# A selective-scan megakernel: GpSimd makes every fourth product of dt*u with B, in place, and those scans read SBUF alone

## The chip, the cores and the metric

One core of one Trainium2 chip. The metric is the device time of one execution in microseconds (us); the median of several executions counts. The times shown here come from three timed executions of the kernel before and from one profiled execution.

## What is computed

The input is eight sequences of 512 tokens with 128 channels, float32. Two layers follow each other for each sequence: a bidirectional Mamba block with a feed-forward part, a gated ternary MLP, an attention layer with low-rank keys and values, and a mixture of eight experts with top-2 gates. The change touches only the recurrence of the Mamba block:

```
def _selective_scan(u, dt, A, Bm, Cm, Dp):
    h0 = jnp.zeros((u.shape[0], D_INNER, D_STATE), u.dtype)

    def step(h, inp):
        u_t, dt_t, B_t, C_t = inp
        dA = jnp.exp(dt_t[:, :, None] * A)
        h = dA * h + (dt_t * u_t)[:, :, None] * B_t[:, None, :]
        y = jnp.einsum('bds,bs->bd', h, C_t)
        return (h, y)
    _, ys = lax.scan(step, h0, (...))
    return ys.transpose(1, 0, 2) + u * Dp
```

It runs once forwards and once backwards in time, each with 256 inner channels and 16 states, so there are 4096 recurrences of 512 steps for each direction and sequence.

## The kernel before, in words

**Units.** 128 recurrences (8 channels with 16 states each) fill the 128 partitions, and the 512 steps lie along the free dimension. That is a unit. A direction has 32 units (NU), a sequence 64 (UNITS). `dt` and `dt*u` are made once for each half of the channels (`dd`), written to a scratch tensor in DRAM (`spread`), and read back once for each unit, spread over the partitions.

**The steps of unit n**, each on its own engine and tied by semaphores:

1. SyncE's queue loads `dt` and `dt*u` into slot n % 6 of `ring` (512 KB, L563), once scan n-6 has ended and so has freed the slot.
2. ScalarE makes the decay exp(A*dt) in place in half 0 of the slot (`decay`, L971).
3. VectorE makes the product of `dt*u` (half 1 of the slot, in SBUF) with B's rows (`ps_brow`, in PSUM) into `ps_in[n % 2]`, in PSUM (`drive`, L1287).
4. VectorE runs the scan over the decay (SBUF) and the product (PSUM) into one of three slots of `hst` (`scan`, L1295). It waits until the read-out of the scan that last used this slot is done.
5. GpSimd multiplies the states by C's rows into one of six slots of `hc` (`read_out`, L1567). It waits for scan n and for the reduction that frees the slot.
6. TensorE sums the 16 states into `ps_y`, four units at a time (`reduce`, L651).

**B's rows.** For each direction ScalarE's queue loads them from `cut` into `brep` (L1030), one buffer in SBUF, after VectorE has copied those of the direction before; VectorE copies them once for each direction into `ps_brow` (L1283). C's rows have two buffers, `crep`.

**The order.** Every engine executes one program in order. What it does for the units (u), the next head of the Mamba block (h), the gates (g), the rest of the layers of the sequence before (r) and the experts of the sequence before that (x) is interleaved by a string for each engine (`ORDER`, and `TURN_ORDER` for the first sequence). In VectorE's string unit n takes two letters: the product n, then the scan n-1. In GpSimd's string a letter u is the read-out n-1. The strings were written out by a planner; the three stages of three sequences run at once, and so a steady period of the loop handles 64 units.

**Before and behind.** The first sequence has no rest and no experts beside it, and transposes weights; after the last scans there is a flush without units.

Of the kernel before, what the change touches and what calls it, by code (L numbers as in the profile page):

```python
# [26 lines left out]
ALU = mybir.AluOpType  # L27
# [3 lines left out]
P = 128  # L31
T = 512
# [4 lines left out]
S = 16  # L37
R = 8
CU = P // S
NJ = 32 // CU  # L40
KC = 4
NU = NH * 16
# [15 lines left out]
def constants():  # L58
# [18 lines left out]
    turned=10, moved=10,  # L77
    xT=1, xkeep=1, z=4, tap=4, conv=12, u=4, xd=2, cut=32, brep=32, crep=32, brow=2, absd=4, expd=4, third=4,
    logd=4, series=4, small=4, log1p=4, dt=4, du=4, bset=2,
    dA=64, dbu=64, scan=64, hc=64, yskip=4, gated=4, resid=2, sq=6, rstd=6, norm=6,  # L80
    s=1, relu=2, a1=4, h0=4, g1=4, g2=4,
    qT=2, kT=4, kz=1, vlat=1, smax=16, split=2, mT=1, pexp=10, rz=2, yT=2,
    x3=1, lg=1, gmax=1, gexp=1, gates=1, ea=16, eh=16, eo=8, acc=8, mv=1, trs=1, outn=1,
# [2 lines left out]


UNITS = 2 * NU
RING, HST = 6, 3
HST_SLOT = [n % HST for n in range(UNITS - 1)] + [1]  # L90

# [137 lines left out]
def later(last):  # L229
# [3 lines left out]

ORDER = dict(
    PE=(
        "xxxxxuxxrxxruxrxhrrxhrurhuxxhrxrrurxhrhrrurxuhhrrurruxxxrxhxhrxhuxrrxhrrrrrrurrrrrrrrrrhrhhuhrurhurxrrhrrrrrru"
        "rxru"),
    ACT=(
        "xxxuuuxxuxuxxuurruuurhuxuxrxurxhruruuuuxrrhuuhruuruuhuxuxrhruuxuxrrhuuuururururxuuuhxhruhrxuhuxrxxrurrruxxrhru"
        "ruxrrrhruxrrruuuuurrhrrhruhurhuuururrurhuurrrrruruur"),  # L240
    DVE=(
        "uxuuxxxurxuxxguuuuuuuuxuxuururxuuxuhrxuuxruuuuuuuuuhrruhuuruhuxuuxruuururuuuuxuuhgruruuuuuuruuuxuuhhuuruuxuuur"
        "uuugrhruuuuhuuxhuuxrruuxxuuruxhxruuuruxururrurruururxrrruruhrxrrurrhuuuhuhururhuruuughuuuruuuruururhruuuuruuur"
        "uuurrruuur"),
    POOL=(
        "ruuxruxrururruxxxrrruxrurxxxurrurrxxuruuuuuuuxuuuxuuuuuruxuurxxruruuxxuruuuxuxrruuxrxxururrrrxxuuurrurrruuuxru"
        "ruruuururuuurrrrrrurruxurrruururur"))
TURN_ORDER = dict(
    PE=(
        "uttttttttththtttthhtuthuthhuuthhuuuhuhuhhthuhuhhuuhuu"),  # L250
    ACT=(
        "utttututtutthutttttutuhtuhuuuuhtuuuhuuhhhuuhuuuututuuuuuuuuuuuuuhuuhuhuuuhhuuuhuuhuuuuhhuuuuuuuuuuuu"),
    DVE=(
        "tuutuutututtuttuuhuututututhtutuuuthuuguhuuuuutuuthuuuuuuuuhhuuuuuguuuhuuuuthuhuuuuuuuuuuuuuuuuuuuuuuuguuuuuuu"
        "hhuuuuuuuhuhuuuuuuuuuhuuuuhuuuuuhuuuuuhuuuguuuuuuuuuuuuuuu"),
    POOL=(
        "uuuuuuuuuuuuuuuuuuuuuuuuuuuuuuuuuuuuuuuuuuuuuuuuuuuuuuuuuuuuuuuu"))

# [38 lines left out]
def two_layer_kernel(nc, a, out):  # L297

    B = a["x"].shape[0]
    with ExitStack() as ctx:  # L300
        def sb(name, shape, dt=F32):
            return ctx.enter_context(nc.sbuf_tensor("sb_" + name, shape, dt))
# [9 lines left out]
        ps_in, ps_brow, ps_y = [bank["in0"], bank["in1"]], bank["brow"], bank["y"]  # L312
# [5 lines left out]
        cut = nc.dram_tensor("cut_dram", [2, 2 * S, T], F32).ap()  # L318
# [51 lines left out]
        u = [sb(f"u{d}", [P, NH, T]) for d in range(2)]  # L370
        sz = [sb(f"sz{d}", [P, NH, T]) for d in range(2)]
        xd = sb("xd", [P, T])
        brep = sb("brep", [P, T])
        crep = [sb(f"crep{d}", [P, T]) for d in range(2)]
        texp = sb("texp", [P, T])
        tsel = sb("tsel", [P, T])
# [64 lines left out]
        sem = {n: ctx.enter_context(nc.semaphore(n)) for n in PER}  # L441
# [491 lines left out]
        def _(act):  # L933
# [54 lines left out]
            def head(at, ahead, d, tab, prev=True):  # L988
                row = at(ahead)

                def full(name):
                    act.wait_ge(sem["full_h"], row("full_h", tab[name][2] + 1))
                    return bank[tab[name][0][0]]

                if d == 0:
                    act.wait_ge(sem["full_h"], row("full_h", HEAD_INDEX["z11"] + 1 - PER["full_h"]))
                    act.wait_ge(sem["xkeep"], row("xkeep", 0))
                    act.activation(xT, full("xT")[:], ACT.Copy).then_inc(sem["xT"], 1)
                    yield
                if d == 0:  # L1000
                    act.wait_ge(sem["gated"], row("gated", 2 - PER["gated"]))
                elif prev:
                    act.wait_ge(sem["full"], at(-1)("full", REST_INDEX["mo1"] + 1))
                for h in range(NH):
                    act.activation(u[d][:, h, :], full(f"xi{d}{h}")[:], ACT.Identity, scale=taps[d][:, h, KC - 1:KC],
                                   bias=cols[d][:, 0, h:h + 1]).then_inc(sem["tap"], 1)
                yield
                table(SILU)
                act.wait_ge(sem["gated"], row("gated", 2 * d - 2))
                for h in range(NH):  # L1010
                    act.activation(sz[d][:, h, :], full(f"z{d}{h}")[:], ACT.Silu).then_inc(sem["z"], 1)
                for h in range(NH):
                    act.wait_ge(sem["conv"], row("conv", 6 * d + 5 + h))
                    act.activation(u[d][:, h, :], u[d][:, h, :], ACT.Silu).then_inc(sem["u"], 1)
                yield
                yield
                act.wait_ge(sem["xd"], row("xd", d + 1))
                act.wait_ge(sem["brep"], row("brep", 16 * d))
                act.wait_ge(sem["crep"], row("crep", 16 * d))
                act.dma_start(cut[d], xd[64 * d + R:64 * d + R + 2 * S, :]).then_inc(sem["cut"], 16)  # L1020
                yield
                for hf in range(NH * d, NH * d + NH):
                    dt_step(row, hf, lambda: full(f"dtp{hf}"))
                    yield
                    act.wait_ge(sem["du"], row("du", hf + 1))
                    act.dma_start(spread[hf], dd[:].rearrange("p a t -> p (a t)")).then_inc(sem["kept"], 16)
                    if hf % NH == 0:
                        act.wait_ge(sem["cut"], row("cut", 16 * (d + 1)))
                        act.wait_ge(sem["brow"], row("brow", d))
                        act.dma_start(brep[:], cut[d, 0:S, :].unsqueeze(1).broadcast_to([S, CU, T])).then_inc(sem["brep"], 16)  # L1030
                        act.wait_ge(sem["hc"], row("hc", NU * d - NU))
                        act.dma_start(crep[d][:], cut[d, S:2 * S, :].unsqueeze(1).broadcast_to([S, CU, T])).then_inc(sem["crep"], 16)
                    yield
# [144 lines left out]
            at = counts(0)  # L1178
# [3 lines left out]
            at = counts(1)  # L1182
# [3 lines left out]
            with act.Fori(0, B - 3) as b:  # L1186
                at = counts(b, 2)
                interleave(ORDER["ACT"], dict(u=units(at), r=rest(at, BODY), x=experts(at, BODY, out_rows(b)), h=heads(at, BODY)))
                table(EXP_LN)
            at = counts(B - 1)  # L1190
            interleave(final(ORDER["ACT"]), dict(u=units(at), r=rest(at, FINAL), x=experts(at, FINAL, out_rows(B - 3)), h=heads(at, FINAL, True, False)))
            at = counts(B)
            interleave(without(ORDER["ACT"], "ugh"), dict(r=rest(at, FLUSH), x=experts(at, FLUSH, out_rows(B - 2))))
            at = counts(B + 1)
# [6 lines left out]
        def _(dve):  # L1201
# [77 lines left out]
            def drive(row, n):  # L1279
                if n % NU == 0:  # L1280
                    dve.wait_ge(sem["brep"], row("brep", 16 * (n // NU + 1)))
                    dve.wait_ge(sem["dbu"], row("dbu", n))
                    dve.tensor_copy(ps_brow[:], brep[:]).then_inc(sem["brow"], 1)  # L1283
                    dve.wait_ge(sem["brow"], row("brow", n // NU + 1))
                dve.wait_ge(sem["scan"], row("scan", n - 1))
                dve.wait_ge(sem[f"ring{n % RING}"], row(f"ring{n % RING}", 16 * (n // RING + 1)))
                dve.tensor_tensor(ps_in[n % 2][:], ring[:, n % RING, 1, :], ps_brow[:], ALU.mult  # L1287
                                  ).then_inc(sem["dbu"], 1)

            def scan(row, n):  # L1290
                dve.wait_ge(sem["dbu"], row("dbu", n + 1))
                dve.wait_ge(sem["dA"], row("dA", n + 1))
                before = [m for m in range(UNITS) if HST_SLOT[m] == HST_SLOT[n]]
                dve.wait_ge(sem["hc"], row("hc", 1 + max([m for m in before if m < n] or [before[-1] - UNITS])))
                dve.tensor_tensor_scan(hst[:, HST_SLOT[n], :], ring[:, n % RING, 0, :], ps_in[n % 2][:], 0.0,  # L1295
                                       ALU.mult, ALU.add).then_inc(sem["scan"], 1)

            def gate(at, ahead, hf, prev):
# [233 lines left out]
            at, turning = counts(0), turned_out()  # L1532
# [7 lines left out]
            at = counts(1)  # L1540
            interleave(without(ORDER["DVE"], "x"), dict(u=units(at, True), g=gates_of(at, True), r=rest(at, SECOND), h=heads(at, SECOND)))
            with dve.Fori(0, B - 3) as b:
                at = counts(b, 2)
                interleave(ORDER["DVE"], dict(u=units(at, True), g=gates_of(at, True), r=rest(at, BODY), x=experts(at, BODY), h=heads(at, BODY)))
            at = counts(B - 1)
            interleave(final(ORDER["DVE"]), dict(u=units(at, True), g=gates_of(at, True), r=rest(at, FINAL), x=experts(at, FINAL), h=heads(at, FINAL, False)))
            at = counts(B)
# [3 lines left out]
            at = counts(B + 1)  # L1551
# [4 lines left out]
        def _(pool):  # L1556
# [5 lines left out]
            def read_out(row, n):  # L1562
                if n % NU == 0:
# [54 lines left out]
            at = counts(B + 1)
# [34 lines left out]
```

## Time and profile before

| what | us |
|---|---|
| median of three timed executions (1953.61 to 1958.84) | 1955.34 |
| time of the profiled execution | 1948.13 |
| its span, first to last instruction | 1946.3 |
| TensorE busy | 1654.4 (85%) |
| VectorE busy | 1541.2 (79%) |
| ScalarE busy | 1114.8 (57%) |
| GpSimd busy | 752.7 (39%) |

Busy times add up over stages with different limits, so the table alone names no bound. In the rows below, PE is TensorE, PEld its weight loads, DVE VectorE, ACT ScalarE and POOL GpSimd. L1287 is line 1287 of the kernel. Durations are us unless marked ns.

### The profile page before, as it was taken

The page shows a single profiled execution, that of the slowest core. Times are in us where ns is not written, and L with a number is a line of the kernel's source. Part 1 is how long each engine was busy: PE and PEld are TensorE (multiplying, and loading weights), DVE is VectorE, ACT ScalarE, POOL GpSimd, SP SyncE. Part 2 cuts the span into 40 slices and gives each one's busy share as a digit, 9 for nine tenths or more (in the row PEclk, how much of TensorE's full clock was granted, in tenths as well). Part 3 has the DMA queues.
Part 4 walks back from the last instruction along what each step waited for, and adds up shares of the span by engine and source line. Part 5 has one row for each costly group of instructions (what it writes and reads, how often), then busy time and mean ns, then how long its engine had stood idle before and what let it go on. Part 6 is the DMA issues. An engine that isn't in the chain of part 4 may idle for free.

```text
span 1946.3 us, 26951 instructions
## 1 busy us (share of the span) xinstructions
PE 1654.4 (85%) x8352; PEld 768.0 (39%) x8352; DVE 1541.2 (79%) x2163; ACT 1114.8 (57%) x1553; POOL 752.7 (39%) x601
## 2 busy tenths in 40 slices
PE   3533588889988999889988999889988999889888
PEld 2200134344444435334444435344444435344545
DVE  3999799779995999779995999779996999631514
ACT  3544486467854885567853885567754884433132
POOL 0455454334632454334632454334533454410102
PEclk7655699999999999999999999999999999989999
DMA  7999998667864896668864796667864896500000
GB/s 187 230 244 248 220 242 203 153 156 199 204 153 121 188 216 163 165 143 196 200 156 118 184 218 163 168 147 198 194 156 112 195 219 165 120 0 0 6 1 6
DMA packets 107915, 309.48 MB, mean 159 GB/s; under 512 B 15970, under 2 KB 32244, under 8 KB 107764
## 3 DMA queue, kind: packets, MB, share of 16 engines
q1 hardware_dynamic: 93556, 279.32, 60.9%
q10 hardware_dynamic: 14208, 28.32, 4.5%
q8 instruction: 74, 1.21, 0.3%
q14 instruction: 77, 0.63, 0.1%
HBM read 287.67 MB, written 19.92 MB: 158 GB/s over the span
## 4 chain that ended last, share of the span: by engine, by line
PE 36%; DVE 28%; issue 13%; ACT 13%; DMA 4%; SPq 2%; ACTq 2%; DVEq 1%; POOL 0%; POOLq 0%
PE ps_pair L716 12%; DVE sb_hst L1295 10%; PE ps_pair L813 7%; DMA sb_ring<-spread_dram 4%; PE ps_pair L872 4%; PE ps_pair L801 4%; DVE ps_in L1287 3%; PE ps_pair L892 3%; ACT sb_mix L1129 3%; DVE sb_nmax L1436 2%; ACT sb_ring L971 2%; ACT L940 2%; DVE sb_u L1339 2%; PE ps_pair L816 1%; DVE sb_eh L1504 1%
## 5 line engine op out<-in xcount | busy, mean ns | idle before, releaser
L1567 POOL TENSOR_TENSOR sb_hc<-sb_hst,sb_crep 128x512 f32<-128x512 f32 x512 | 652.8, 1284 | 916.2 <-DVE sb_hst L1295 642.0
L1295 DVE TENSOR_TENSOR_SCAN sb_hst<-sb_ring,ps_in 128x512 f32<-128x512 f32 x512 | 620.0, 1211 | 5.0 <-ACT sb_ring L971 2.5
L971 ACT ACTIVATE sb_ring<-sb_ring,sb_A 128x512 f32<-128x512 f32 x512 | 344.8, 713 | 207.6 <-DMA sb_ring<-spread_dram 116.9
L1287 DVE TENSOR_TENSOR ps_in<-sb_ring,ps_brow 128x512 f32<-128x512 f32 x512 | 354.4, 692 | 29.5 <-DMA sb_ring<-spread_dram 11.5
L940 ACT ACT_TABLE_LOAD x181 | 232.2, 1283 | 46.4 <-issue 39.4
L872 PE MATMUL ps_pair<-sb_mix,sb_ew 128*128 128x512 f32 x512 | 250.0, 624 | 4.6 <-ACT sb_ea L1163 2.2
L651 PE MATMUL ps_y<-sb_hc,sb_const 128*32 128x512 f32 x1024 | 154.2, 678 | 98.8 <-POOL sb_hc L1567 68.7
L813 PE MATMUL ps_pair<-sb_g,sb_h 128*128 128x512 f32 x320 | 168.6, 652 | 15.8 <-DVE sb_dd L1275 5.1
L801 PE MATMUL ps_pair<-sb_h,sb_g 128*128 128x512 f32 (+3 forms) x512 | 165.0, 452 | 13.1 <-DVE sb_nmax L1436 7.8
L872 PEld LDWEIGHTS ps_pair<-sb_mix,sb_ew 128*128 128x128 f32 x512 | 96.6, 198 | 139.1 <-issue 95.3
L892 PEld LDWEIGHTS ps_pair<-sb_ew,sb_eh 128*128 128x128 f32 x1024 | 121.6, 192 | 26.2 <-issue 17.8
L1600 POOL TENSOR_TENSOR sb_mix<-sb_mix 128x512 f32<-128x512 f32 x56 | 71.2, 1272 | 155.8 <-DVE sb_mix L1512 154.9
L892 PE MATMUL ps_pair<-sb_ew,sb_eh 128*128 128x128 f32 x1024 | 124.0, 276 | 1.3 <-DVE sb_xn L1382 0.6
L716 PE MATMUL ps_pair<-sb_h,sb_h1T 128*128 128x512 f32 x256 | 115.5, 605 | 2.5 <-DVE sb_h L1404 2.5
L716 PE MATMUL ps_pair<-sb_g,sb_h2T 128*128 128x512 f32 x256 | 115.5, 605 | 0.0
L1129 ACT ACTIVATE sb_mix<-ps_pair 128x1024 f32<-128x1024 f32 x56 | 57.2, 1022 | 98.1 <-PE ps_pair L820 62.4
L1436 DVE TENSOR_REDUCE sb_nmax<-ps_pair 128x2 f32<-128x256 f32 (+3 forms) x128 | 102.3, 815 | 11.3 <-PE ps_pair L804 10.5
L801 PEld LDWEIGHTS ps_pair<-sb_h,sb_g 128*128 128x128 f32 x512 | 82.0, 190 | 55.7 <-issue 21.7
L1504 DVE TENSOR_TENSOR sb_eh<-ps_pair,sb_ea 128x512 f32<-128x512 f32 x128 | 83.1, 680 | 25.1 <-PE ps_pair L872 23.6
L651 PEld LDWEIGHTS ps_y<-sb_hc,sb_const 128*32 128x32 f32 x1024 | 21.8, 113 | 194.7 <-POOL sb_hc L1567 104.0
L813 PEld LDWEIGHTS ps_pair<-sb_g,sb_h 128*128 128x128 f32 x320 | 57.2, 199 | 96.2 <-issue 47.7
L1163 ACT ACTIVATE sb_ea<-ps_pair 128x512 f32<-128x512 f32 x128 | 70.7, 597 | 29.9 <-PE ps_pair L872 29.2
(219 smaller groups left out, 2065.0 us busy)
## 6 DMA issues: line engine op xcount, KB each, us to landing
sb_ring<-spread_dram SPq DMA_DIRECT2D x512, 512.0 KB, 5.9
spread_dram<-sb_dd ACTq DMA_DIRECT2D x32, 512.0 KB, 3.7
sb_brep<-cut_dram ACTq DMA_DIRECT2D x16, 256.0 KB, 4.1
sb_crep<-cut_dram ACTq DMA_DIRECT2D x16, 256.0 KB, 4.1
sb_xtok<-in_L_attn_x_dram SPq DMA_DIRECT2D x8, 256.0 KB, 6.0
sb_ew<-in_L_ffn_w_dram SPq DMA_DIRECT2D x2, 1024.0 KB, 14.0
out_dram<-sb_yy ACTq DMA_DIRECT2D x8, 256.0 KB, 2.3
sb_h<-in_L_ffn_h_w_dram SPq DMA_DIRECT2D x1, 1024.0 KB, 8.9
```

The source lines that it names most:

```text
L651: ins = pe.matmul(ps_y[32 * q:32 * q + 32, :], red, hc[:, (4 * k + q) % 6, :], start=(j == 0), stop=(j == 3))
L716: ins = pe.matmul(o[:], l, r, start=(i == 0), stop=(i == len(lhs) - 1))
L801: pe.matmul(ps_pair[i % 2][:, k, 0:(t + 1) * P], qT[:, tl, r, :], kz[:, 2 * k + hf, 0:(t + 1) * P], start=True, stop=False)
L813: pe.matmul(ps_pair[0][:, hf, :], kz[:, 2 * k + hf, j * P:(j + 1) * P], qT[:, TILES[hf].index(t), :, :], start=True, stop=False)
L872: ins = pe.matmul(o[:], l, r, start=(i == 0), stop=(i == len(lhs) - 1))
L892: ins = pe.matmul(o[:, n * D:(n + 1) * D], eh[:, e % 2, c, n * P:(n + 1) * P], ew2[:, e, c, :], start=(c == 0), stop=(c == 1))
L940: act.preload_act_table_set(name)
L971: act.activation(ring[:, n % RING, 0, :], ring[:, n % RING, 0, :], ACT.Exp, scale=A[d][:, g:g + 1]).then_inc(sem["dA"], 1)
L1287: dve.tensor_tensor(ps_in[n % 2][:], ring[:, n % RING, 1, :], ps_brow[:], ALU.mult).then_inc(sem["dbu"], 1)
L1295: dve.tensor_tensor_scan(hst[:, HST_SLOT[n], :], ring[:, n % RING, 0, :], ps_in[n % 2][:], 0.0, ALU.mult, ALU.add).then_inc(sem["scan"], 1)
L1436: dve.tensor_reduce(nmax[:, tl, r, :, hf], ps_pair[i % 2][:, :, 0:(t + 1) * P], AX.X, ALU.max, negate=True).then_inc(sem["smax"], 1)
L1567: pool.tensor_tensor(hc[:, n % 6, :], hst[:, HST_SLOT[n], :], crep[n // NU][:], ALU.mult).then_inc(sem["hc"], 1)
```

## The change

Of the 64 products of a sequence, those of units 3, 7, 11, ... 63 (`POOLED`) go to GpSimd. It multiplies half 1 of the ring slot by `brep`, in place, both in SBUF. The scan of such a unit reads its decay and its product from the ring slot, both in SBUF. The other 48 products stay on VectorE, with `ps_brow` and `ps_in` in PSUM. In GpSimd's program the product of unit n+1 stands ahead of the read-out of unit n-1. `brep` gets two buffers, one for each direction, and their loads wait in addition for the products of the sequence before (`pbu`). The order strings of all engines are new (a pooled unit's first letter u in VectorE's string does nothing any more, except for the copy of B's rows).

```diff
-    dA=64, dbu=64, scan=64, hc=64, yskip=4, gated=4, resid=2, sq=6, rstd=6, norm=6,
+    dA=64, dbu=48, pbu=16, scan=64, hc=64, yskip=4, gated=4, resid=2, sq=6, rstd=6, norm=6,
...
+POOLED = [n % 4 == 3 for n in range(UNITS)]
...
     DVE=(
-        "uxuuxxxurxuxxguuuuuuuuxuxuururxuuxuhrxuuxruuuuuuuuuhrruhuuruhuxuuxruuururuuuuxuuhgruruuuuuuruuuxuuhhuuruuxuuur"
-        "uuugrhruuuuhuuxhuuxrruuxxuuruxhxruuuruxururrurruururxrrruruhrxrrurrhuuuhuhururhuruuughuuuruuuruururhruuuuruuur"
-        "uuurrruuur"),
+        "uxxuuxxuxurguxuuuuuuuuuxuxxururxuuxuuurhuruhuuxuuuururuuhuuuxxuhrxruururxruuuuuugruuuurrhuuxuuuuxhuruuuuuurh"
+        "uuuugurrhuxuuhuruuuxuuxrxuxruhhhxuuruuuxururrurrurururrxrxrrrururhuuuhuhuruuruuuhughuuuuuurruuruurrrururuuhru"
+        "uuuruuruur"),
...
-        brep = sb("brep", [P, T])
+        brep = [sb(f"brep{d}", [P, T]) for d in range(2)]
...
                         act.wait_ge(sem["brow"], row("brow", d))
-                        act.dma_start(brep[:], cut[d, 0:S, :].unsqueeze(1).broadcast_to([S, CU, T])).then_inc(sem["brep"], 16)
+                        act.wait_ge(sem["pbu"], row("pbu", sum(POOLED[:NU * (d + 1)]) - sum(POOLED)))
+                        act.dma_start(brep[d][:], cut[d, 0:S, :].unsqueeze(1).broadcast_to([S, CU, T])).then_inc(sem["brep"], 16)
...
             def drive(row, n):
                 if n % NU == 0:
                     dve.wait_ge(sem["brep"], row("brep", 16 * (n // NU + 1)))
-                    dve.wait_ge(sem["dbu"], row("dbu", n))
-                    dve.tensor_copy(ps_brow[:], brep[:]).then_inc(sem["brow"], 1)
+                    dve.wait_ge(sem["dbu"], row("dbu", n - sum(POOLED[:n])))
+                    dve.tensor_copy(ps_brow[:], brep[n // NU][:]).then_inc(sem["brow"], 1)
                     dve.wait_ge(sem["brow"], row("brow", n // NU + 1))
+                if POOLED[n]:
+                    return
                 dve.wait_ge(sem["scan"], row("scan", n - 1))
...
             def scan(row, n):
-                dve.wait_ge(sem["dbu"], row("dbu", n + 1))
+                if POOLED[n]:
+                    dve.wait_ge(sem["pbu"], row("pbu", sum(POOLED[:n]) + 1))
+                    dbu = ring[:, n % RING, 1, :]
+                else:
+                    dve.wait_ge(sem["dbu"], row("dbu", n + 1 - sum(POOLED[:n])))
+                    dbu = ps_in[n % 2][:]
...
-                dve.tensor_tensor_scan(hst[:, HST_SLOT[n], :], ring[:, n % RING, 0, :], ps_in[n % 2][:], 0.0,
+                dve.tensor_tensor_scan(hst[:, HST_SLOT[n], :], ring[:, n % RING, 0, :], dbu, 0.0,
                                        ALU.mult, ALU.add).then_inc(sem["scan"], 1)
...
+            def drive(row, n):
+                if n % NU <= 3:
+                    pool.wait_ge(sem["brep"], row("brep", 16 * (n // NU + 1)))
+                pool.wait_ge(sem[f"ring{n % RING}"], row(f"ring{n % RING}", 16 * (n // RING + 1)))
+                pool.tensor_tensor(ring[:, n % RING, 1, :], ring[:, n % RING, 1, :], brep[n // NU][:], ALU.mult
+                                   ).then_inc(sem["pbu"], 1)
+
             def units(at, prev):
                 for n in range(UNITS):
+                    if n + 1 < UNITS and POOLED[n + 1]:
+                        drive(at(0), n + 1)
                     if n >= 1:
                         read_out(at(0), n - 1)
```

## Rows read from the trace of the kernel before

**Rows 1.** The page: the chain that ended last, by engine
```profile
PE 36%; DVE 28%; issue 13%; ACT 13%; DMA 4%; SPq 2%; ACTq 2%; DVEq 1%; POOL 0%; POOLq 0%
```

**Rows 2.** Busy time by stretch: PE, PEld, DVE, ACT, POOL, then PEclk, DMA share, GB/s
```profile
46.00:206.00 160.00, 64.10 (x237) 21.10 (x239) 152.46 (x192) 74.14 (x111) 81.60 (x64) 0.60 0.97 237
874.00:1030.00 156.00, 146.06 (x645) 67.00 (x645) 150.03 (x207) 105.91 (x148) 75.50 (x60) 0.98 0.76 185
1030.00:1092.00 62.00, 54.41 (x388) 25.42 (x386) 40.00 (x58) 34.38 (x47) 18.07 (x15) 0.97 0.58 138
874.00:1092.00 218.00, 200.47 (x1032) 92.42 (x1031) 190.03 (x265) 140.29 (x195) 93.57 (x74) 0.98 0.71 171
```

**Rows 3.** The page: groups of instructions (busy us, mean ns, idle before them and releaser)
```profile
L1567 POOL TENSOR_TENSOR sb_hc<-sb_hst,sb_crep 128x512 f32<-128x512 f32 x512 | 652.8, 1284 | 916.2 <-DVE sb_hst L1295 642.0
L1295 DVE TENSOR_TENSOR_SCAN sb_hst<-sb_ring,ps_in 128x512 f32<-128x512 f32 x512 | 620.0, 1211 | 5.0 <-ACT sb_ring L971 2.5
L1287 DVE TENSOR_TENSOR ps_in<-sb_ring,ps_brow 128x512 f32<-128x512 f32 x512 | 354.4, 692 | 29.5 <-DMA sb_ring<-spread_dram 11.5
```

**Rows 4.** Timeline, VectorE, around two units that follow each other closely
```profile
906.80 0.68 DVE L1287 TENSOR_TENSOR ps_in<-sb_ring,ps_brow 128x512 f32<-128x512 f32 x1
907.40 1.21 DVE L1295 TENSOR_TENSOR_SCAN sb_hst<-sb_ring,ps_in 128x512 f32<-128x512 f32 x1
908.64 0.70 DVE L1287 TENSOR_TENSOR ps_in<-sb_ring,ps_brow 128x512 f32<-128x512 f32 x1
909.25 1.21 DVE L1295 TENSOR_TENSOR_SCAN sb_hst<-sb_ring,ps_in 128x512 f32<-128x512 f32 x1
```

**Rows 5.** Timeline, GpSimd, the same stretch
```profile
908.77 1.26 POOL L1567 TENSOR_TENSOR sb_hc<-sb_hst,sb_crep 128x512 f32<-128x512 f32 x1 [2.44 <-DVE sb_hst L1295]
```

**Rows 6.** One line's instructions (L1384), by operands: duration ns min/median/max
```profile
L1384 DVE TENSOR_TENSOR sb_g<-ps_pair,sb_res x8: 690/692/692, 228.7 to 1737.5; 128x512 f32<-128x512 f32 x8
L1384 DVE TENSOR_TENSOR sb_xn<-sb_res,sb_rstd x8: 692/1734/1740, 314.4 to 1812.0; 128x512 f32<-128x512 f32 x8
L1384 DVE TENSOR_TENSOR sb_mix<-sb_res,sb_rstd x8: 693/1681/1683, 409.1 to 1891.5; 128x512 f32<-128x512 f32 x8
```

**Rows 7.** Timeline, VectorE and GpSimd, around one such instruction
```profile
744.36 1.74 DVE L1384 TENSOR_TENSOR sb_xn<-sb_res,sb_rstd 128x512 f32<-128x512 f32 x1
...
744.28 1.26 POOL L1600 TENSOR_TENSOR sb_mix<-sb_mix 128x512 f32<-128x512 f32 x1
```

**Rows 8.** Timeline, VectorE and GpSimd: a GpSimd instruction that begins after VectorE's
```profile
1093.60 0.69 DVE L1391 TENSOR_TENSOR sb_g<-sb_g 128x512 f32<-128x512 f32 x1
...
1093.66 1.77 POOL L1600 TENSOR_TENSOR sb_mix<-sb_mix,sb_yy 128x512 f32<-128x512 f32 x1
```

**Rows 9.** One line's instructions (L1600), in place, both operands in SBUF
```profile
L1600 POOL TENSOR_TENSOR sb_mix<-sb_mix x56: 1261/1272/1287, 439.6 to 1939.2; 128x512 f32<-128x512 f32 x56
```

**Rows 10.** Waits from 874 to 1092 us, by engine (us in total, times, longest)
```profile
POOL sb_hc L1567 <- DVE sb_hst L1295: 75.4, 37, 10.4
POOL sb_hc L1567 <- PE ps_y L651: 39.0, 8, 12.4
PEld ps_y L651 <- POOL sb_hc L1567: 7.4, 6, 3.2
DVE sb_yy L1447 <- ACT sb_rstd L1137: 9.1, 1, 9.1
DVE sb_g L1447 <- ACT sb_rstd L1137: 6.0, 1, 6.0
DVE ps_brow L1283 <- issue: 3.4, 1, 3.4
```

**Rows 11.** The ring's loads (L563), whole run: issue to landing
```profile
DMA to landing us min/median/max: 4.2/5.9/17.6
```

More of the change, by code:

```diff
@@ L235 @@
     PE=(
-        "xxxxxuxxrxxruxrxhrrxhrurhuxxhrxrrurxhrhrrurxuhhrrurruxxxrxhxhrxhuxrrxhrrrrrrurrrrrrrrrrhrhhuhrurhurxrrhrrrrrru"
-        "rxru"),
+        "xxxxxxuxrxxruxrxhrurxhrurhxxhuxrrrrxhrrrurhuxhhrrrurxhuxrxhxrxxhxurrhxurrrrrrrrrrrrrrrrhhxxrhhururhurrrrrrhrrr"
+        "urur"),
     ACT=(
-        "xxxuuuxxuxuxxuurruuurhuxuxrxurxhruruuuuxrrhuuhruuruuhuxuxrhruuxuxrrhuuuururururxuuuhxhruhrxuhuxrxxrurrruxxrhru"
-        "ruxrrrhruxrrruuuuurrhrrhruhurhuuururrurhuurrrrruruur"),
+        "uxxxxuxuxxuxuuururuurxhxuuxururxhruruuuxhuxururururhhxuururhururuuuhuxrruururxuxxuuhrhuhuruhrurxxurxrxrhxrrrxr"
+        "ruuuurrrruurxhxrrurrhhruhuruhruurruuuururhrrruurruur"),
     DVE=(
-        "uxuuxxxurxuxxguuuuuuuuxuxuururxuuxuhrxuuxruuuuuuuuuhrruhuuruhuxuuxruuururuuuuxuuhgruruuuuuuruuuxuuhhuuruuxuuur"
-        "uuugrhruuuuhuuxhuuxrruuxxuuruxhxruuuruxururrurruururxrrruruhrxrrurrhuuuhuhururhuruuughuuuruuuruururhruuuuruuur"
-        "uuurrruuur"),
+        "uxxuuxxuxurguxuuuuuuuuuxuxxururxuuxuuurhuruhuuxuuuururuuhuuuuxxuhrxruururxruuuuuugruuuurrhuuxuuuuuxhuruuuuuurh"
+        "uuuugurrhuxuuhuruuuxuuxrxuxruhhhxuuruuuxururrurrurrururrxrxrrrururhuuuhuhuruuruuuhughuuuuuurruuruurrrururuuhru"
+        "uuuruuruur"),
     POOL=(
-        "ruuxruxrururruxxxrrruxrurxxxurrurrxxuruuuuuuuxuuuxuuuuuruxuurxxruruuxxuruuuxuxrruuxrxxururrrrxxuuurrurrruuuxru"
-        "ruruuururuuurrrrrrurruxurrruururur"))
+        "uxxruuuruuurrxxrrxrurxruuuruxuuuxrrruuuxuuuuuurruxxrrxruuuuuuxxxuuxuuruxxurruurrxrrxrrurrrrrrurxxurrruxrrurrrr"
+        "xurxrrruuuxuruuuxururuuurruuuuruuu"))
 TURN_ORDER = dict(
     PE=(
-        "uttttttttththtttthhtuthuthhuuthhuuuhuhuhhthuhuhhuuhuu"),
+        "ttttttthhtuhthuttthtuhtuhthttuuhuuthuhuhhuuthhuhuhhuu"),
     ACT=(
-        "utttututtutthutttttutuhtuhuuuuhtuuuhuuhhhuuhuuuututuuuuuuuuuuuuuhuuhuhuuuhhuuuhuuhuuuuhhuuuuuuuuuuuu"),
+        "utttuttutthhuuutuuttuuuuuhthhutuhttuuutuuhuuuuutuhhuuuuuhtuuuuuuuhuuuhuuhuuuhuhuuuuuuhtuuuuhuuuhuuuu"),
     DVE=(
-        "tuutuutututtuttuuhuututututhtutuuuthuuguhuuuuutuuthuuuuuuuuhhuuuuuguuuhuuuuthuhuuuuuuuuuuuuuuuuuuuuuuuguuuuuuu"
-        "hhuuuuuuuhuhuuuuuuuuuhuuuuhuuuuuhuuuuuhuuuguuuuuuuuuuuuuuu"),
+        "tttuuttuuhuuututuhutuuuuhutuuttuuhuutuuuuuuuhguuuuuthtutuuuutuuuuuuuhhhuuuguuuuuutuuuuuuuuuutuuuuguuuuuuuuhuuu"
+        "huuhuuuuuuuuuuuhuhuuuuuuhuuuuuuuuuuguuuuuuuhuhuuuuhuuuuuuu"),
     POOL=(
```

## The prediction

> **What bounds the kernel now.** I read the chain of waits first, then the stretches, then the waits of one period. The chain [rows 1] has TensorE first with 36%, VectorE second with 28%, and GpSimd with nothing. So VectorE's work is on the path about a third of the time: 28% of the span of 1946.3 us is 545 us, out of 1541.2 us in which it is busy, a share of 0.35. The stretches [rows 2] show where. From 46 to 206 us, the first sequence, VectorE is busy 95% of the time, but the DMA engines 97%: whoever makes VectorE faster there meets the loads of the ring. From 874 to 1030, most of a steady period, VectorE is busy 150.0 of 156 us and TensorE 146.1: both nearly full, neither alone the bound. From 1030 to 1092 VectorE is busy 40 of 62 and waits: 9.1 and 6.0 us for the attention's reciprocals and 3.4 us for B's rows [rows 10]. Over the whole period of 218 us TensorE has 200.5 us of work, VectorE 190.0, GpSimd 93.6. The last 240 us have no units and do not change.
>
> **What is taken from VectorE.** 16 products in a sequence. One lasts 692 ns [rows 3], but the scan behind it starts 0.60 us after it (906.80 to 907.40, [rows 4]), so 0.60 us is what it costs in VectorE's order. 16 x 0.60 = 9.6 us a period.
>
> **What GpSimd gets.** 16 products in place. The nearest row is its addition in place over the same shape, 1272 ns [rows 9]: 16 x 1.27 = 20.4 us. It goes from 93.6 to 114 us of 218, 52%, and is still far from full as a mean.
>
> **The scans with both inputs in SBUF.** No row shows one. First its own duration: a multiplication lasts 692 ns with one input in PSUM and 692 to 693 ns at the least with both in SBUF [rows 6], so the form costs nothing by itself, and I keep 1.21 us [rows 3]. Then the neighbour: the same multiplication has a median of 1734 and 1681 ns [rows 6], and the timeline tells why. One begins at 744.36, while GpSimd is at work from 744.28 to 745.54 [rows 7], and takes 1.74 us: 1.05 more than alone, with 1.18 us of GpSimd's instruction left. It waits for all of it but 0.13 us. The other way round it is the same: GpSimd's addition begins at 1093.66, just behind a VectorE instruction with two SBUF inputs, and takes 1.77 us in place of 1.27 [rows 8]. The Trainium skill states it as a rule (SBUF — State Buffer, "Who interferes with whom"): a VectorE instruction with two SBUF inputs and a GpSimd instruction that reads SBUF exclude each other for a whole instruction. By that rule, the trace agrees, the change gives away what the PSUM buffers of the kernel before had bought; without it the sum below would be 5.7 us a period better.
>
> How often does a pooled scan meet GpSimd at work? In a tight sequence (scan n-1, product n+1, scan n) always: the scan before ends at 908.61, GpSimd begins its read-out at 908.77 and ends at 910.03, and the next scan begins at 909.25 [rows 4, 5]. 0.78 us are left, so the wait would be 0.65 us, a little more than the 0.60 us that the product's removal brings. Such a unit gains nothing. In VectorE's new order I count for the 16 pooled scans what stands between scan n-1 and scan n: 4 (n = 3, 27, 31, 47) have only a product there, and 12 have one or more further letters, each of which can carry an instruction of some 0.6 us or more, after which the read-out is over unless GpSimd is behind. For these 12 I take GpSimd's share of 0.52 times half of its duration less the 0.13: 0.52 x 0.5 = 0.26 us each. Sum: 4 x 0.65 + 12 x 0.26 = 5.7 us. The bounds are 0 (all meet it idle) and 16 x 1.14 = 18.2 us (each meets one that has just begun). I take the value near the lower end since GpSimd waits 75.4 us in the period for scans [rows 10], so that it is mostly idle when a scan ends.
>
> So VectorE is relieved by 9.6 - 5.7 = 3.9 us a period; the bounds are +9.6 and -8.6.
>
> **What of it reaches the end.** By the share of 0.35 it is 1.4 us a period. In seven sequences behind the first that is 9.6 us. In the first sequence the DMA engines leave free 3% of 160 us, 4.8 us [rows 2], and the relief is 3.9 us: between 0 and 3.9 us can come of it, and I take 0.4, since the loads of the ring set the pace there. The sum is 10 us.
>
> **What costs nothing, and what covers it.** Two buffers for B's rows: the load for a direction now waits for the pooled products of the same direction one sequence back, which are over for half a sequence or more; should the added wait block ScalarE's queue, the load of C's rows and the decays stand behind it. GpSimd's new wait for the ring slot: product n stands ahead of read-out n-2. Its load is issued when scan n-6 ends and lands 5.9 us later [rows 11]; read-out n-2 could begin at the end of scan n-2, four units later, at the closest 4 x 1.84 = 7.4 us (906.80 to 908.64, [rows 4]). So 1.5 us of cover; if a load takes over 7.4 us, the read-out stands behind a load that it does not need, and behind it TensorE's reduction. The loads of the ring are freed by scans as before. The 16 GpSimd read-outs held up by a pooled scan get up to 1.08 us later; GpSimd has 75 us of waits for scans to take that up. New order strings move steps of every engine; I give them nothing, and plus or minus 6 us in the range.
>
> **The time.** The profiled execution took 1948.13 us, its span 1946.3. The sum would make that 1938.1. The median shown is 1955.34, 7.2 us above the profiled one; against it the forecast is 1955.34 - 10 = 1945.3, so 1945. About 0.3% (6 us) is what a measurement of this kernel can tell from no change.
>
> **The rivals.**
>
> *Same (chance 0.22).* TensorE holds 200.5 of 218 us, and its order is fixed; what VectorE gains, TensorE doesn't pick up. For it: TensorE is first in the chain. Against: it is idle 10 us from 874 to 1030, more than the relief. Time: 1953 (1950 to 1960).
>
> *The exclusion costs more than the product (0.16), slower.* In a stretch with close units GpSimd has five instructions for four units, 5 x 1.27 = 6.35 us, and can't work during the pooled scan, 1.08 more: 7.4 us, where VectorE needed 4 x 1.84 = 7.4 before. It no longer catches up after one of its 8 waits for a reduction [rows 10], and then pooled scans meet it at work each time. It decides from 9.6 / 16 = 0.60 us of wait for each pooled scan. At 1.0 us each VectorE has 6.4 us more a period; nearly full from 874 to 1030, it passes on half: 3.2 x 8 = 26. Time: 1981; at 0.8 us each 1968. Against it: the new order sets other work ahead of 12 of the 16 scans.
>
> *GpSimd late for TensorE (0.16), slower.* TensorE already waits 6 times and 7.4 us a period for read-outs [rows 10]. A product of 1.27 us ahead of a read-out that a reduction waits for lengthens that wait by as much: 6 x 1.27 = 7.6 us, half of it unless VectorE's relief covers it, 3.8 - 1.4 = 2.4 us a period, 8 times: 19. Time: 1974. It decides from 1.4 us more of TensorE's waits a period. The Trainium skill says (GPSIMD Engine Reference, "Performance versus the Vector engine") that GpSimd is about two times slower at such a product; 1272 against 692 ns [rows 9, 3] is 1.84.
>
> *A larger gain* is part of the forecast: no scan waits and 0.6 of 9.6 us is on the path, since VectorE is 96% busy in that stretch: 5.8 x 7 = 40, of which TensorE's 10 us of gaps let through perhaps 30: 1925.
>
> **How the numbers follow.** The forecast, faster by over 0.3%, has 0.46. Same has 0.22 and the two slower rivals 0.32 together. The range leaves out 2 in 10: from 1924 (the larger gain) to 1976 (the third rival, and the second up to 0.9 us a scan). The forecast's own range is 1924 to 1949.
>
> **What would show it.** The products on VectorE number 384 in place of 512, and GpSimd has 128 new ones of 1.27 us at the median. The scans fall into two groups: those with both inputs in SBUF have a minimum of 1.21 us, and a mean of 1.57 by my sum (1.21 + 5.7 / 16), which is the number to look at: above 1.81 the change has cost VectorE more than it took away. The steady period goes from 218 to 216.6 us. TensorE's waits for read-outs should stay near 7.4 us a period; the third rival has them above 11. The first sequence keeps its length. The forecast is wrong if the mean of the pooled scans is above 1.81, if TensorE's waits grow, or if the period shrinks by more than 4 us.

## The result and the profile after

The changed kernel takes 1998.22 us at the median (1995.78 to 2003.30, four executions) against 1955.43 of the kernel before: a ratio of 1.022, 95% interval 1.0194 to 1.0246. It is slower, where the forecast was 1945 and the range ended at 1976. The profiled execution took 1999.89 us, its span 1998.1.

The page of the changed kernel, busy times:

```profile
PE 1674.7 (84%) x8352; PEld 779.6 (39%) x8352; DVE 1508.4 (75%) x2035; ACT 1108.3 (55%) x1547; POOL 923.2 (46%) x729
```

VectorE is busy 32.8 us less than the 1541.2 before, GpSimd 170.5 more, TensorE 20.3 more for the same 8352 matrix multiplications, and in the profiled executions the end comes 52 us later. Over the span TensorE was granted a mean clock of 0.924 of its full speed, against 0.932 before. The page, groups of instructions, as in [rows 3]:

```profile
L1576 POOL TENSOR_TENSOR sb_hc<-sb_hst,sb_crep 128x512 f32<-128x512 f32 x512 | 667.4, 1312 | 852.4 <-DVE sb_hst L1304 601.7
L1304 DVE TENSOR_TENSOR_SCAN sb_hst<-sb_ring,ps_in 128x512 f32<-128x512 f32 x384 | 459.5, 1210 | 95.7 <-ACT sb_ring L972 92.6
L1291 DVE TENSOR_TENSOR ps_in<-sb_ring,ps_brow 128x512 f32<-128x512 f32 x384 | 266.1, 693 | 28.6 <-DMA sb_ring<-spread_dram 13.9
L1304 DVE TENSOR_TENSOR_SCAN sb_hst<-sb_ring 128x512 f32<-128x512 f32 x128 | 189.4, 1480 | 38.8 <-ACT sb_ring L972 36.1
L1583 POOL TENSOR_TENSOR sb_ring<-sb_ring,sb_brep 128x512 f32<-128x512 f32 x128 | 163.3, 1276 | 7.3 <-DMA sb_ring<-spread_dram 7.3
```

The change is made as told: 384 products on VectorE, 128 of 1276 ns on GpSimd. The 128 scans with two inputs in SBUF have a mean of 1480 ns against 1210, so they wait 0.27 us each on average, 34.6 us in all, or 4.3 us a period. The prediction had 5.7. New is the idle time ahead of the scans: 128.7 us of waits for ScalarE's decays (92.6 and 36.1), where [rows 3] have 2.5.

How a pooled scan meets GpSimd (timelines of VectorE and of GpSimd, one tight sequence):

```profile
885.59 0.70 DVE L1291 TENSOR_TENSOR ps_in<-sb_ring,ps_brow 128x512 f32<-128x512 f32 x1
886.20 1.80 DVE L1304 TENSOR_TENSOR_SCAN sb_hst<-sb_ring 128x512 f32<-128x512 f32 x1
...
884.43 2.49 POOL L1576 TENSOR_TENSOR sb_hc<-sb_hst,sb_crep 128x512 f32<-128x512 f32 x2 [0.45 <-DVE sb_hst L1304]
```

GpSimd's second read-out ends at 886.92, 0.72 us after the scan's start, and the scan takes 1.80, 0.59 more than alone: 0.72 less 0.13, as in [rows 7].

The stretches, with the columns of [rows 2] (the steady period now goes from 879 to 1104 us):

```profile
46.00:206.00 160.00, 65.73 (x232) 20.74 (x234) 147.43 (x177) 73.93 (x110) 103.58 (x80) 0.58 0.99 236
879.00:1104.00 225.00, 201.45 (x1032) 94.10 (x1031) 187.11 (x249) 139.38 (x194) 115.70 (x90) 0.97 0.69 167
```

The first sequence kept its length, with the DMA engines at 99%: its last scan ends at 204.4 us, before at 204.2. The loss is in the loop: a period of 225 us in place of 218, with as much work for TensorE (201.45 against 200.47) and less for VectorE. The waits in it (from 879 to 1104 us):

```profile
POOL sb_hc L1576 <- DVE sb_hst L1304: 75.9, 35, 11.5
POOL sb_hc L1576 <- PE ps_y L652: 33.4, 7, 11.9
DVE sb_hst L1304 <- ACT sb_ring L972: 16.7, 5, 8.0
PEld ps_y L652 <- POOL sb_hc L1576: 9.5, 6, 4.5
ACT L941 <- POOL sb_hc L1576: 7.5, 1, 7.5
PE ps_y L652 <- POOL sb_hc L1576: 5.7, 3, 3.7
DVE ps_brow L1285 <- issue: 3.8, 1, 3.8
DVE sb_yy L1456 <- ACT sb_rstd L1139: 1.5, 1, 1.5
```

Against [rows 10], VectorE's wait of 9.1 us for the attention's reciprocal is 1.5 now, and 16.7 us before scans are new. TensorE's waits for read-outs went from 7.4 to 9.5 us in its weight loads, and in its multiplications to 5.7 us. Before it was (874 to 1092 us):

```profile
PE ps_y L651 <- POOL sb_hc L1567: 0.5, 1, 0.5
```

None of this says which part of the change costs what.

### The profile page after: what moved, and what is told of

It reads as the page before. It is cut to its first block, busy times and chain, and to the rows that moved or that the text cites. A ratio compares the mean times of both kernels' runs of the same rounds, so it can differ in the third digit from the quotient of the medians.

```text
span 1998.1 us, 27212 instructions
## 1 busy us (share of the span) xinstructions
PE 1674.7 (84%) x8352; PEld 779.6 (39%) x8352; DVE 1508.4 (75%) x2035; ACT 1108.3 (55%) x1547; POOL 923.2 (46%) x729
## 3 DMA queue, kind: packets, MB, share of 16 engines
q8 instruction: 74, 1.21, 0.3%
## 4 chain that ended last, share of the span: by engine, by line
PE 29%; DVE 8%; issue 6%; ACT 6%; POOL 2%; DMA 0%; DVEq 0%; ACTq 0%; POOLq 0%
PE ps_pair L717 8%; PE ps_pair L873 5%; PE ps_pair L814 4%; PE ps_pair L802 3%; PE ps_pair L893 3%; DVE sb_hst L1304 3%; POOL sb_hc L1576 1%; ACT sb_mix L1131 1%; PE ps_y L652 1%; ACT sb_ring L972 1%; PE ps_pair L817 1%; PE ps_pair L670 1%; ACT L941 1%; DVE sb_nmax L1445 1%; ACT sb_g L1131 1%
## 5 line engine op out<-in xcount | busy, mean ns | idle before, releaser
L1576 POOL TENSOR_TENSOR sb_hc<-sb_hst,sb_crep 128x512 f32<-128x512 f32 x512 | 667.4, 1312 | 852.4 <-DVE sb_hst L1304 601.7
L1304 DVE TENSOR_TENSOR_SCAN sb_hst<-sb_ring,ps_in 128x512 f32<-128x512 f32 x384 | 459.5, 1210 | 95.7 <-ACT sb_ring L972 92.6
L1291 DVE TENSOR_TENSOR ps_in<-sb_ring,ps_brow 128x512 f32<-128x512 f32 x384 | 266.1, 693 | 28.6 <-DMA sb_ring<-spread_dram 13.9
L652 PE MATMUL ps_y<-sb_hc,sb_const 128*32 128x512 f32 x1024 | 155.5, 682 | 129.0 <-POOL sb_hc L1576 106.9
L873 PE MATMUL ps_pair<-sb_mix,sb_ew 128*128 128x512 f32 x512 | 256.7, 639 | 5.8 <-DVE sb_g L1393 3.1
L1304 DVE TENSOR_TENSOR_SCAN sb_hst<-sb_ring 128x512 f32<-128x512 f32 x128 | 189.4, 1480 | 38.8 <-ACT sb_ring L972 36.1
L1583 POOL TENSOR_TENSOR sb_ring<-sb_ring,sb_brep 128x512 f32<-128x512 f32 x128 | 163.3, 1276 | 7.3 <-DMA sb_ring<-spread_dram 7.3
L717 PE MATMUL ps_pair<-sb_g,sb_h2T 128*128 128x512 f32 x256 | 122.2, 634 | 5.0 <-DVE sb_dd L1277 3.1
L1513 DVE TENSOR_TENSOR sb_eh<-ps_pair,sb_ea 128x512 f32<-128x512 f32 x128 | 83.7, 683 | 40.7 <-PE ps_pair L873 39.4
L1618 POOL TENSOR_TENSOR sb_mix<-sb_mix 128x512 f32<-128x512 f32 x56 | 75.5, 1348 | 56.2 <-DVE sb_mix L1521 55.3
```

Of the source, the lines that this page charges most:

```text
L652: ins = pe.matmul(ps_y[32 * q:32 * q + 32, :], red, hc[:, (4 * k + q) % 6, :], start=(j == 0), stop=(j == 3))
L717: ins = pe.matmul(o[:], l, r, start=(i == 0), stop=(i == len(lhs) - 1))
L873: ins = pe.matmul(o[:], l, r, start=(i == 0), stop=(i == len(lhs) - 1))
L1583: pool.tensor_tensor(ring[:, n % RING, 1, :], ring[:, n % RING, 1, :], brep[n // NU][:], ALU.mult).then_inc(sem["pbu"], 1)
```

## The experiments

The change has four parts: VectorE is relieved (relief), GpSimd is loaded (load), 128 scans read SBUF twice (exclusion), and all order strings are new (order). The first theory was that load and exclusion cost it; the rival, that the order does. Each ratio is to the kernel before, run on the same chip.

| run | order | products of the 16 units by | their scans' inputs | ratio (95%) | us |
|---|---|---|---|---|---|
| relief_old | old | nobody | one in SBUF | 0.994 (0.992 to 0.996) | 1941.57 |
| nolock_old | old | GpSimd | one in SBUF | 1.003 (1.001 to 1.005) | 1960.27 |
| old_order | old | GpSimd | two in SBUF | 1.020 (1.017 to 1.022) | 1988.82 |
| lock_old | old | VectorE | two in SBUF | 1.016 (1.014 to 1.017) | 1982.24 |
| load_old | old | VectorE, and an idle one on GpSimd | one in SBUF | 1.007 (1.005 to 1.010) | 1962.03 |
| delay_old | old | VectorE | one in SBUF, 0.3 us later | 1.014 (1.011 to 1.017) | 1980.43 |
| order_only | new | VectorE | one in SBUF | 1.029 (1.027 to 1.030) | 2006.22 |
| relief_new | new | nobody | one in SBUF | 1.011 (1.005 to 1.016) | 1970.76 |
| nolock_new | new | GpSimd | one in SBUF | 1.010 (1.007 to 1.013) | 1969.95 |
| the change | new | GpSimd | two in SBUF | 1.022 (1.019 to 1.025) | 1998.22 |

**The order alone.** The kernel before with the new strings:

```diff
 ORDER = dict(
-        "xxxxxuxxrxxruxrxhrrxhrurhuxxhrxrrurxhrhrrurxuhhrrurruxxxrxhxhrxhuxrrxhrrrrrrurrrrrrrrrrhrhhuhrurhurxrrhrrrrrru"
+        "xxxxxxuxrxxruxrxhrurxhrurhxxhuxrrrrxhrrrurhuxhhrrrurxhuxrxhxrxxhxurrhxurrrrrrrrrrrrrrrrhhxxrhhururhurrrrrrhrrr"
...
```

> The kernel before with nothing but the new order strings; all 64 products stay on VectorE. Theory O (the new order is worse by itself: the steady period went from 218 to 225.7 us although VectorE is busy 33 us less in the run): about 1990 us, a steady period of 224 to 226. Theory L (GpSimd's load and the exclusion between it and VectorE make the loss, the order is as good as the old one): 1950 to 1962. Theory M (the new strings are cut to the new costs, so that with 64 products on VectorE they are worse than with 48): above 2005.

Measured: 1.029, 55 us more. The new order is slower by itself, and with 64 products it is even slower than the change. That is theory M's figure (above 2005), and L's "as good as the old one" falls. From its waits, the whole run:

```profile
DVE sb_hst L1295 <- ACT sb_ring L971: 105.0, 30, 7.4
ACT L940 <- POOL sb_hc L1567: 30.3, 4, 8.0
```

ScalarE, which makes the decays, waits for read-outs itself ahead of its table loads (the second row). The scans' waits for decays come with the strings, not with GpSimd's products, which this kernel does not have.

**The change in the old order.** The strings of the kernel before put into the changed kernel.

> The change with the order strings of the kernel before. Theory O: the relief of VectorE shows at last, 1935 to 1955 us. Theory L: as slow as the changed kernel, 1990 to 2005, since the pooled scans wait and the read-outs are late whatever the order. Theory M: slower still than the changed kernel, since the old strings do not know the new costs, above 2005.

Measured: 1.020 (1988.82 us, just below theory L's range), and the interval overlaps that of the change. So with all the rest of the change in place, the new strings cost 0.2%, which is not clear of nothing; without them there is a loss of the same size, of another make.

**The exclusion alone.**

```diff
-                dve.tensor_tensor(ps_in[n % 2][:], ring[:, n % RING, 1, :], ps_brow[:], ALU.mult
+                dve.tensor_tensor(ring[:, n % RING, 1, :] if POOLED[n] else ps_in[n % 2][:], ring[:, n % RING, 1, :], ps_brow[:], ALU.mult
...
+                dbu = ring[:, n % RING, 1, :] if POOLED[n] else ps_in[n % 2][:]
```

> Old order, all 64 products on VectorE, but those of units 3, 7, ... are written in place into the ring, and these 128 scans read both inputs from SBUF; nothing is added to GpSimd. It measures the exclusion alone. From the overlay of the trace of before, 10 of 16 such scans would begin inside a read-out, with 6.7 us left in sum a period, so 5 us of waits a period on VectorE; if they reach the end by half (the share of the forecast was 0.35 to 0.6) it is 1955 + 8 x 2.5 = 1975. Theory L: 1975 to 1995. Theory O: below 1970.

Measured: 1.016, 31 us. Its groups, the scans:

```profile
L1297 DVE TENSOR_TENSOR_SCAN sb_hst<-sb_ring,ps_in 128x512 f32<-128x512 f32 x384 | 465.4, 1212 | 5.4 <-ACT sb_ring L972 2.6 <-POOL sb_hc L1569 2.1 <-DVE ps_in L1288 0.6
L1297 DVE TENSOR_TENSOR_SCAN sb_hst<-sb_ring 128x512 f32<-128x512 f32 x128 | 195.0, 1523 | 0.9
```

Each of the 128 scans is 0.31 us longer, 5.0 us a period, and the end comes 31.4 / 8 = 3.9 us a period later: four fifths of it, not a third. TensorE's granted clock (0.931) is that of before, so this loss does not come by the clock.

**GpSimd's load alone.**

```diff
+                    if n + 1 < UNITS and n % 4 == 2:
+                        pool.wait_ge(sem[f"ring{(n + 1) % RING}"], at(0)(f"ring{(n + 1) % RING}", 16 * ((n + 1) // RING + 1)))
+                        pool.tensor_tensor(junk[:], junk[:], junk[:], ALU.mult)
```

> The kernel before, with 16 idle multiplications a sequence added on GpSimd (a buffer of zeros with itself, same shape), at the places and behind the ring waits that the pooled products have; VectorE as before. It measures GpSimd's load alone: read-outs late by up to 1.27 us. If GpSimd's lateness reaches TensorE (third rival of the prediction) 1965 to 1975; if GpSimd has room (39% busy before) within 0.3% of 1955.

Measured: 1.007, 11 us, between the two figures expected. It is not shown to be GpSimd's lateness. From 870 to 1090 us TensorE waits as before for read-outs, 7.4 us in its loads and 0.5 in its multiplications. Its page, busy times:

```profile
PE 1652.8 (84%) x8312; PEld 767.9 (39%) x8352; DVE 1552.5 (79%) x2163; ACT 1113.9 (57%) x1553; POOL 885.9 (45%) x730
```

VectorE has the same instructions and is busy 11.3 us longer (1541.2 before): its other instructions with two SBUF inputs meet the added ones. The mean of the predicated copy of the dt steps went from 874 to 1002 ns. How the 11 us divide is open.

**The relief alone, in the old order.** The 16 products are left out, so the scans of these units have a wrong input (against the changed kernel):

```diff
-                    dbu = ring[:, n % RING, 1, :]
+                    dbu = ps_in[n % 2][:]
...
-                    if n + 1 < UNITS and POOLED[n + 1]:
-                        drive(at(0), n + 1)
```

> Old order; the products of units 3, 7, ... are left out altogether (their scans read an earlier product from PSUM), GpSimd makes none. It measures what 9.6 us a period less on VectorE is worth in the old order. If the share on the path is the 0.35 of the prediction: 1951 - 7 x 3.4 = 1927 us. If VectorE's relief is worth nothing because the order and TensorE hold the period: 1945 to 1955. If the stretch is bound by VectorE wholly: 1890.

Measured: 0.994, 12 us less than its 1953.85 beside it (1927 was expected of a share of 0.35, 1945 or more of none). That is 1.5 us a period for 9.6 us of VectorE's time, a share of 0.16; by the interval it is 0.10 to 0.19. In the profiled execution the last scan of the first sequence ends at 197.9 us, 6.3 us earlier than before.

**The change less the exclusion, in the old order.** Only the first two lines of the edit above: GpSimd multiplies, the scans read PSUM.

> Old order; GpSimd makes the 16 products as in the change, but the scans of these units read an earlier product from PSUM, so that no scan has two SBUF inputs (the recurrences of those units get a wrong input). The difference to old_order (1989) is the exclusion, to relief_old the load on GpSimd. If the exclusion costs as much as in lock_old (31 us): 1957. If relief shows: relief_old plus 11 us. If the old order's loss has another cause than the exclusion (GpSimd's products late because of the ring wait): above 1975.

Measured: 1.003, 1960.27 us, close to the 1957 expected if the exclusion costs as in lock_old. The load costs 0.9% here (1.003 less 0.994) and the exclusion 1.7% (1.020 less 1.003). The load's part is again more than lateness for TensorE: VectorE is busy 11.2 us longer than in relief_old (1480.2 against 1469.0), and its scans wait 13.2 us for GpSimd's products.

**The same two in the new order.**

> New order; 16 products left out altogether as in relief_old, none on GpSimd. If the new order is good once VectorE is relieved and nothing excludes (it was planned so): below relief_old, 1925 or less. If the new order is worse by itself: above relief_old by 20 us or more.

> The changed kernel with its own order, but the scans of the pooled units read an earlier product from PSUM: the change less the exclusion. If the exclusion is the main loss: 1955 to 1970 (1998 less 31). If the order is the main loss, the exclusion matters little here, where other work stands ahead of 12 of the 16 scans and the measured waits are 0.27 us a scan: 1985 to 1995.

Measured: 1.011 and 1.010. With the same work on all engines, the new order is 1.6% slower than the old (1.0105 against 0.9942). The load costs nothing measurable in it (the intervals are 1.005 to 1.016 and 1.007 to 1.013), and the exclusion 1.2% (1.022 against 1.0097). Of nolock_new the figure for the exclusion as the main loss came true at its upper end (1969.95 of 1955 to 1970): the exclusion costs 24 us. The pages of relief_old and relief_new, busy times:

```profile
PE 1651.7 (85%) x8352; PEld 766.2 (40%) x8352; DVE 1469.0 (76%) x2035; ACT 1113.4 (58%) x1553; POOL 751.7 (39%) x601
PE 1680.8 (86%) x8352; PEld 782.6 (40%) x8352; DVE 1460.5 (74%) x2035; ACT 1108.4 (56%) x1547; POOL 745.2 (38%) x601
```

TensorE does the same work and is busy 29.1 us longer, nearly the whole difference of the two spans (1933.1 and 1964.6). The granted clock goes with it: a mean of 0.934 against 0.921, and the single executions of the two kernels do not overlap (0.929 to 0.935, 0.915 to 0.925). So a lower clock of TensorE is one way in which the new strings can cost time; no run here separates it as cause from consequence.

The order's cost depends on the rest of the kernel. New against old strings is 2.9% with all products on VectorE, 1.6% with the relief, 0.7% with relief and load (1.010 against 1.003), and 0.2% with the exclusion too (1.022 against 1.020).

The first sequence ends its last scan at 197.6 us in nolock_new, where the change has 204.4. And TensorE's multiplications wait 106.9 us for read-outs in the whole run of the change, but 70.5 in nolock_new and 68.7 before. These are one profiled execution each. By them, in the new order both the late read-outs and the unchanged first sequence come with the exclusion and not with GpSimd's load.

**Why relief brings little and waits cost much.** A copy of 240 columns from PSUM ahead of the 16 scans:

```diff
+                if n % 4 == 3:
+                    dve.tensor_copy(junk[:, 0:240], ps_brow[:, 0:240])
```

> The kernel before, with a short copy of 240 columns from ps_brow (PSUM) into a spare buffer ahead of each scan of units 3, 7, ...: 16 more instructions of some 0.3 us a period on VectorE, about the 0.31 us by which lock_old lengthened these scans, with one PSUM input each and so without any exclusion. If VectorE's lost time by itself is what the exclusion costs (VectorE is on the path when it gets slower, though not when it gets faster): 1.012 to 1.018 of before. If the share of 0.35 of the prediction holds both ways: 1.006 to 1.008. If the exclusion costs through GpSimd, whose read-outs wait for the scans: below 1.006.

Measured: 1.014 (1.011 to 1.017), where lock_old has 1.016 (1.014 to 1.017). In its trace the scan starts 0.32 us after the copy, 40.7 us in all for the 128, of which 26.7 reach the end (1980.43 less 1953.73), a share of 0.66. VectorE's lost time by itself costs as much as the exclusion within the noise; no detour over GpSimd is needed to explain it. TensorE's granted clock was a little lower than in lock_old (0.925 against 0.931), so the 0.66 may hold some of that. The chains that ended last, on the pages of relief_old and of lock_old, one line each; before, it was PE 36%, DVE 28% [rows 1] (the chains of the kernels with all strings new are not used: that of the change breaks off at half the span):

```profile
PE 55%; DVE 15%; ACT 12%; issue 8%; DMA 6%; SPq 2%; ACTq 1%; DVEq 0%; POOL 0%; POOLq 0%
```

```profile
PE 32%; DVE 32%; issue 15%; ACT 12%; DMA 4%; SPq 2%; DVEq 1%; ACTq 1%; POOL 0%; POOLq 0%
```

With VectorE relieved, the path moves to TensorE and VectorE's share halves; with VectorE slowed, it grows. A period of relief_old, 217 us long (columns of [rows 2]), has the same 200.6 us of TensorE's work and leaves VectorE more idle:

```profile
857.00:1074.00 217.00, 200.57 (x1033) 92.60 (x1032) 181.25 (x250) 140.56 (x195) 93.70 (x74) 0.98 0.71 173
```

**Which string it is.** Three kernels without the change's products mix old and new strings: new_PE has TensorE's new string alone, new_DVE VectorE's alone (both but for the first sequence), and old_PE has all new but TensorE's.

> The kernel before with the new order string of TensorE alone (steady and last sections), the others old. If TensorE's new sequence makes the loss of order_only (1.029): 1.015 or more. If another engine's string makes it: 1.000 to 1.008. A misfit between strings can only add.

> order_only (all strings new, 1.029) with TensorE's old string put back. If TensorE's string makes the loss: 1.000 to 1.012. If another one makes it: 1.025 or more.

> The kernel before with the new order string of VectorE alone. The new string is written for 48 products: if it is the one that loses (it puts further letters between the scans where the product of a pooled unit is gone), 1.015 or more; if not, 1.000 to 1.008.

Measured: new_PE 1.023 (1.020 to 1.026), old_PE 1.068 (1.066 to 1.071), new_DVE 1.077 (1.074 to 1.079). TensorE's new string alone loses 2.3%, with only 2.9 us of scans waiting for decays, so such waits are not needed for a loss. But the other two kernels lose far more than all new strings together, so misfit between strings outweighs what was sought. The strings work as a set; no single one is shown to be the cause.

**Picked units.** The old order, with GpSimd making 11 products where it was idle in the trace of before:

```diff
-POOLED = [n % 4 == 3 for n in range(UNITS)]
+POOLED = [n in (1, 8, 11, 12, 20, 22, 40, 44, 47, 60, 63) for n in range(UNITS)]
```

> Old order; GpSimd makes 11 products in place of 16, for the units 1, 8, 11, 12, 20, 22, 40, 44, 47, 60 and 63: in the steady periods of the trace of before their scans begin outside a read-out, and GpSimd is idle for 1.3 us or more where the product goes. If the exclusion and the load are what the change costs in the old order (1.0198: relief -0.6%, load +0.9%, exclusion +1.7%), both fall away and two thirds of the relief are left: 0.994 to 0.999 of before. If the loss comes with each product whatever its place: 11/16 of the loss, 1.012 to 1.015.

Measured: 1.0016 (1.0004 to 1.0027), 1955.73 us. Nearly all of the loss of old_order is gone, against 1.012 to 1.015 expected if it came with each product, but the 0.994 to 0.999 expected if nothing but relief were left is missed. Its groups and GpSimd's waits show two things that are left:

```profile
L1304 DVE TENSOR_TENSOR_SCAN sb_hst<-sb_ring 128x512 f32<-128x512 f32 x88 | 126.3, 1435 | 1.8 <-DVE sb_mix L1490 1.5 <-POOL sb_ring L1583 0.2
```

```profile
POOL sb_ring L1583 <- DMA sb_ring<-spread_dram: 62.7, 10, 44.3
```

The scans still wait 0.22 us each (1435 ns against 1212), probably since the units no longer stand where the old trace had them once the products are moved. And GpSimd waits for ring loads with read-outs behind it: 44.3 of the 62.7 us are before the very first load and cost nothing, the other nine waits are 18.4 us.

A version with the decay of the pooled units in PSUM, so that their scans have one SBUF input and a right product, was not run. No kernel with the reference's result beat the kernel before.

## Why the prediction was wrong, and where it held

**The share of 0.35** is the step that fails whichever strings the kernel has. It was read off the chain as VectorE's part of the path, and the net relief of 9.6 - 5.7 = 3.9 us was multiplied by it, so relief and waits had one price. Relief is worth 0.16 of its time (relief_old), added time 0.66 to 0.79 (delay_old, and lock_old with 31.4 us of 39.8). The exclusion in the change itself fits: 24 us of the 34.6 that its scans wait, about 0.7. The row for it was there: from 874 to 1030 TensorE is busy 146.1 and VectorE 150.0 of 156 us [rows 2]. With two engines that level, less work on one hands the path to the other, and more work on one is mostly path. The prediction read it as "neither alone the bound" and took the mean of two slopes.

**The exclusion** was right as a mechanism and roughly as a size: 0.27 us a scan measured, 0.36 predicted, and the 0.13 us of overlap held. It was priced 9.6 - 5.7 = 3.9 us a period to the good. At the measured shares it is 9.6 x 0.16 = 1.5 gained against 4.3 x 0.66 to 0.79, 2.8 to 3.4, lost: slower, by 10 to 15 us in eight periods. Not counted were other VectorE instructions with two SBUF inputs that meet a busier GpSimd: the mean of one in the steps for dt went from 818 to 1133 ns, and GpSimd's 16 products lengthen VectorE's busy time by 11 us in either order even where no scan is excluded. The rule of the Trainium skill (SBUF — State Buffer, "Who interferes with whom") spoke against the change, and lock_old agrees: 1.016.

**The order strings** ("I give them nothing, and plus or minus 6 us in the range") are the second step that failed, a term put at nothing without a reason. Alone they cost 2.9% (order_only), with the relief 1.6% (relief_new against relief_old), and with everything else of the change in place 0.2%, within the noise (the change against old_order). Counted first, they are the largest loss in the change; counted last, they are next to none, since in the old order the load (0.9%) and a larger exclusion (1.7%, 0.40 us a scan) take as much. So no single figure is the cost of the order in the change. What in the strings costs stays open: with all of them new, VectorE's scans wait for decays (105.0 us in order_only) and TensorE's granted clock is lower (0.918 against 0.932), but new_PE loses 2.3% almost without the first.

**The rival of the exclusion** named the right mechanism with a wrong point of decision: it was to decide above 0.60 us a scan, the break-even of VectorE's busy time. It costs 24 us at 0.27. For the same reason the sign of being wrong, a mean above 1.81 us, did not show at 1.48.

**GpSimd late for TensorE** was to show as waits above 11 us a period. TensorE's load waits are 9.5, and its multiplications wait 5.7 more, where they waited 0.5. So the sign is there if both are counted, but its cause is not the extra instruction ahead of the read-outs: without the exclusion the same load leaves the waits as they were (nolock_new) and costs nothing measurable.

**What held:** the tail kept its length, the product on GpSimd took 1276 ns, and the double buffer of B's rows cost nothing that a trace shows. The first sequence kept its length too, but not for the reason given. The prediction let the ring's loads hold it, with 3.9 us at most to gain; relief_old and nolock_new end it 6 to 7 us earlier, so in the change the waits of the pooled scans took that gain away.

One way from before to the change, in its own order, is relief -0.6%, order +1.6%, load 0, exclusion +1.2%, in all 2.2%; in the old order it is relief -0.6%, load +0.9%, exclusion +1.7%, order +0.2%. Each is a chain of differences that must end at the measured figure, so its fit proves nothing; that the parts differ shows how far they depend on each other.

## What to carry to other kernels

Where two engines are equally full in a stretch, price relief and added waits by different slopes: here a gain counted for a sixth, a wait for two thirds or more, and an exchange of one for the other loses even if the busy time falls. Count a wait from a second SBUF input against GpSimd mostly as path time there. If a change brings a new static order, run the old kernel in the new order and the new kernel in the old one: the first lost 2.9% here and the second 2.0%, and together they show that the parts don't add.

## What the runs showed of the hardware

The scan obeys the same exclusion as the multiplication in [rows 6]. One with both inputs in SBUF that began at 886.20 us, inside a GpSimd instruction that ended at 886.92, ended 1.08 us after that one; all such scans of lock_old that began with more than 0.2 us of a GpSimd instruction left did so within 0.01 us. It takes about 1.22 us when GpSimd is idle, nearly the same as with an input in PSUM (1.21). The other side is held up too: the read-outs' mean went from 1284 to 1312 ns in the change.
